# Joining the two recurrences of a bidirectional WKV layer into one scan, and moving the gate product one chunk later

## The reference, cut to what matters

```python
def step(carry, kv_t):                      # per channel, along T = 16384 tokens
    p, q, o = carry
    no = jnp.maximum(o, u + kt)
    A = jnp.exp(o - no); Bw = jnp.exp(u + kt - no)
    y = (A * p + Bw * vt) / (A * q + Bw)
    no2 = jnp.maximum(w + o, kt)
    A2 = jnp.exp(w + o - no2); B2 = jnp.exp(kt - no2)
    return ((A2 * p + B2 * vt, A2 * q + B2, no2), y)
...
k = jnp.einsum('btc,dc->btd', xs, Wk); v = ...Wv; r = ...Wr
x_fwd = wkv_scan(real_w, u, k, v)
x_bwd = jnp.flip(wkv_scan(real_w, u, jnp.flip(k, 1), jnp.flip(v, 1)), 1)
h = jax.nn.sigmoid(r) * 0.5 * (x_fwd + x_bwd)
h = layernorm(h) * ln_g + ln_b
out = jnp.einsum('btc,dc->btd', h, Wo)
```

## Time and profile before

| | us |
|---|---|
| median of 3 runs | 7379.21 |
| lowest, highest | 7375.27, 7381.88 |
| the profiled execution, its own time | 7389.65 |
| its span (first to last instruction) | 7388.1 |

### The profile page before, as it was taken

How to read it: one execution, slowest core, us unless ns; L and a number is a source line. 1 busy time by engine, 2 the same in 40 slices (tenths; PEclk the granted TensorE clock), 3 DMA queues, 4 the chain that set the end, 5 groups by cost and what they waited for, 6 DMA issues and landing times. The chain is left out here.

```text
span 7388.1 us, 83141 instructions
## 1 busy us (share of the span) xinstructions
PE 5742.4 (78%) x25278; PEld 2350.9 (32%) x25278; DVE 5654.6 (77%) x5545; ACT 2765.0 (37%) x3703; POOL 350.0 (5%) x553
## 2 busy tenths in 40 slices
PE   0999997999999564556665777688678879986888
PEld 0333332433333464333332222222222223222222
DVE  6333333999999777888885666599889979997998
ACT  0222222211111574111110000055479965546998
POOL 0111100000000000222220000000000000000000
PEclk9999999999999776777777877789789988877999
DMA  7556565999999996999997999644366644445665
GB/s 293 194 178 201 176 200 167 277 273 271 268 274 264 228 230 147 246 248 251 251 249 178 265 261 264 180 187 183 151 215 230 230 157 179 182 172 191 224 230 181
DMA packets 1208246, 1615.57 MB, mean 219 GB/s; under 512 B 87300, under 2 KB 907205, under 8 KB 1194693
## 3 DMA queue, kind: packets, MB, share of 16 engines
q1 hardware_dynamic: 865733, 1314.24, 59.3%
q10 hardware_dynamic: 314880, 201.39, 9.9%
q0 software_dynamic: 27520, 98.54, 5.2%
HBM read 1006.55 MB, written 607.33 MB: 218 GB/s over the span
## 5 line engine op out<-in xcount | busy, mean ns | idle before, releaser
L508 PE MATMUL dw_p<-dw_it,dw_tt 128*128 128x512 f32 x2304 | 1024.8, 606 | 122.6 <-DVE dw_tt L424 84.5
L547 DVE SCALAR_TENSOR_TENSOR dw_vo<-dw_vi,keep_wv,dw_vo 128x2048 f32<-128x2048 f32 x384 | 903.1, 2352 | 13.6
L842 PE MATMUL bc_p<-bc_z,bc_wc 128*32 128x256 f32 x9216 | 572.3, 414 | 399.9 <-DVE bc_z L881 399.9
L320 PE MATMUL pw_p<-pw_xh,pw_wlo 128*112 128x512 f32 x1536 | 693.2, 601 | 184.0 <-POOL pw_xh L274 184.0
L881 DVE STREAM_TRANSPOSE bc_z<-bc_xp 128x1536 f32<-128x1536 f32 x256 | 710.8, 2842 | 155.3 <-DMA bc_xp<-d 154.6
L1090 PE MATMUL ap_p<-ap_vt,ap_pw 96*96 96x512 f32 x1024 | 592.7, 744 | 191.5 <-DMA ap_xt<-in_x 187.0
L508 PEld LDWEIGHTS dw_p<-dw_it,dw_tt 128*128 128x128 f32 x2304 | 441.4, 193 | 706.1 <-issue 671.2
L525 ACT ACTIVATE dw_ot<-dw_p 128x512 f32<-128x512 f32 x384 | 215.6, 599 | 931.5 <-PE dw_p L508 663.7
L375 DVE COPY pw_ut<-pw_p 112x512 f32<-112x512 f32 x384 | 247.3, 686 | 379.5 <-PE pw_p L326 377.5
L842 PEld LDWEIGHTS bc_p<-bc_z,bc_wc 128*32 128x32 f32 x9216 | 323.9, 119 | 648.4 <-issue 486.5
L820 ACT ACTIVATE bc_xt<-bc_p 128x256 f32<-128x256 f32 x384 | 147.8, 385 | 873.9 <-PE bc_p L842 873.9
(11 more groups left out here) (313 smaller groups left out, 9826.6 us busy)
## 6 DMA issues: line engine op xcount, KB each, us to landing
u<-pw_ut SPq DMA_DIRECT2D x64, 2240.0 KB, 12.7
dw_it<-u SPq DMA_DIRECT2D x192, 512.0 KB, 10.8
d<-dw_ot ACTq DMA_DIRECT2D x192, 512.0 KB, 12.1
gr_qk<-d SPq DMA_DIRECT2D x128, 768.0 KB, 9.1
bc_xp<-d SPq DMA_DIRECT2D x256, 288.0 KB, 12.1
bc_xp<-d POOLq DMA_DIRECT2D x256, 288.0 KB, 9.9
gs_xt<-in_x SPq DMA_DIRECT2D x24, 2048.0 KB, 7.2
d<-dw_vo SPq DMA_DIRECT2D x96, 512.0 KB, 8.6
```

Of the source, the lines that this page charges most:

```text
L320: mm(pt[m % NBANK][e][:, :], wlo[:, wm], xh[:, h, 2 * e, cols], start=True, stop=False, skip_group_check=True)
L508: mm = nc.tensor.matmul(po[c][:, :].rearrange("p (b w) -> p b w", b=B), tt[:, h, 3 * c + dx, 0:H], it[:, h, B * c:B * (c + 1), dx:dx + W], ...
L547: nc.vector.scalar_tensor_tensor(vo[:, h], src, w, vo[:, h], ALU.mult, ALU.add).then_inc(tapped, 1)
L842: mm = nc.tensor.matmul(po[q % NBANK][32 * c4:32 * c4 + 32, :, :], wc[:, c, dx, :, :].rearrange("p j r -> p (j r)"), z[:, h, c, :, dx:dx + ...
```

## The change

In both functions the denominator's and the numerator's terms now lie in one buffer, [128, 3 tiles, 2, 512]: `bb` replaces `bl` and `bvl`, `fb` replaces `bf` and `bvf` and has one extra column per row (pitch 513), `sums` replaces `qq` and `pp`, `dn` replaces `den` and `num`. `ewt` holds the decay written out in full, [128, 3, 2, 513], with 0 in the extra column.

- One scan per chunk runs over all 6 x 513 = 3078 columns. At each extra column the factor 0 wipes the running value out and the carried start value is added in its place. One product of 6 columns replaces the two of `carry`.
- The sums with the bonus are three instructions of 2 x 512 columns. The rescaling on ACT is three ACTIVATEs of 2 x 512 columns.
- Backward: ACT evacuates `pv` with the bias added (three more ACTIVATEs), DVE multiplies b x v in SBUF instead of reading PSUM, and the bias matmuls (six pieces per chunk) go. b and b x v go to HBM with one DMA of twice the size, and forward loads them with one.
- The order of DVE's step changes: the scan, then y and b x v (backward) or `var`, the clamp, and the gate product of the chunk before (forward), and `dn` last.
- Forward: `rc`, y, the gate product `hh` and 1/den are handled for chunk n-2 in step n (before: n-1); `var`, `rs` and hh x rs for n-3 (before: n-2); the evacuation of `po` for n-4 (before: n-3). On ACT 1/den comes first, and exp(-r) nearly last. PE's order changes likewise: r, the residual, the mean of chunk n-2, the projection of n-3, the mean of the squares of n-2.

The core of the diff:

```diff
+def row(ap):
+    return ap.rearrange("p a b t -> p (a b t)")
+def spread_decay(nc, dve, ewt, ew, slot, spread):
+    for tile in range(3):
+        last = nc.vector.tensor_copy(ewt[:, tile].rearrange("p b t -> p (b t)"), ew[:, tile, :].to_broadcast([128, 2 * CH + 2]))
+    last.then_inc(spread, 1)
+    dve.wait_ge(spread, 1)
+    nc.vector.memset(ewt[:, :, :, slot:slot + 1], 0.0).then_inc(spread, 1)
+    dve.wait_ge(spread, 2)
+def carry(nc, dve, m, slots, ends, factor, scanned, carried):
+    if isinstance(m, int) and m == 0:
+        nc.vector.memset(slots, 0.0).then_inc(carried, 1)
+    else:
+        dve.wait_ge(scanned, m)
+        nc.vector.tensor_tensor(slots, ends, factor.rearrange("p (t a) -> p t a", a=1).to_broadcast([128, 3, 2]),
+                                ALU.mult).then_inc(carried, 1)
+    dve.wait_ge(carried, m + 1)
...
# wkv_backward, SP
-                    sp.dma_start(rows_of(b_d, c), flat(bl[:, h])).then_inc(b_stored[h], 16)
...
-                    sp.dma_start(rows_of(bv_d, c), flat(bvl[:, h])).then_inc(bv_stored[h], 16)
+                    sp.dma_start(rows_of(bb_d, chunk(n - 2)), bb[:, h].rearrange("p a b t -> p (a b t)")).then_inc(b_stored[h], 16)
...
# wkv_backward, PE
-                wait(pe, bv_done, n)
-                for tile in range(3):
-                    mm(pv[:, tile, :], vrow[:, tile, :], ones[:, :], start=True, stop=False, skip_group_check=True)
-                project(nc, pv, wv, xt[:, h], begin=False).then_inc(v_done, 1)
+                wait(pe, vv_done, n)
+                project(nc, pv, wv, xt[:, h]).then_inc(v_done, 1)
...
# wkv_backward, ACT (between fac and the rescaling)
+                    act.wait_ge(v_done, n + 1)
+                    for tile in range(3):
+                        last = nc.scalar.activation(bb[:, h, tile, 1, :], pv[:, tile, :], ACT.Identity, bias=vb[:, tile:tile + 1])
+                    last.then_inc(vv_done, 1)
                     act.wait_ge(f_done, n + 1)
                     act.wait_ge(b_done, n + 1)
+                    act.wait_ge(bv_done, n + 1)
+                    wait(act, dn_done, n - 1)
                     for tile in range(3):
-                        last = nc.scalar.activation(bf[:, h, tile, :], bl[:, h, tile, :], ACT.Copy, scale=fac[:, h, 1, tile:tile + 1])
...
+                        last = nc.scalar.activation(fb[:, h, tile, :, 0:CH], bb[:, h, tile, :, :], ACT.Copy,
+                                                    scale=fac[:, h, 1, tile:tile + 1])
...
# wkv_backward, DVE, after diff
+                if has(n, 1):
+                    dve.wait_ge(f_done, n)
+                    dve.wait_ge(fb_done, n)
+                    carry(nc, dve, n - 1, fb[:, g, :, :, CH], sums[:, :, :, 0], fac[:, g, 0, :], scanned, carried)
+                    wait(dve, dn_done, n - 1)
+                    nc.vector.tensor_tensor_scan(row(sums[:, :, :, :])[:, ::-1], row(ewt[:, :, :, :])[:, ::-1], row(fb[:, g])[:, ::-1],
+                                                 ewt[:, 2, 1, CH:CH + 1], ALU.mult, ALU.add).then_inc(scanned, 1)
                 if has(n, 2):
                     dve.wait_ge(rc_done, n - 1)
...
+                    nc.vector.tensor_tensor(yb[:, h], dn[:, :, 1, :], rc[:, :, :], ALU.mult).then_inc(y_done, 1)
+                if has(n):
+                    dve.wait_ge(vv_done, n + 1)
+                    dve.wait_ge(b_done, n + 1)
+                    nc.vector.tensor_tensor(bb[:, h, :, 1, :], bb[:, h, :, 1, :], bb[:, h, :, 0, :], ALU.mult).then_inc(bv_done, 1)
                 if has(n, 1):
...
+                        last = nc.vector.scalar_tensor_tensor(dn[:, tile], fb[:, g, tile, :, 0:CH], eu[:, tile, :],
+                                                              sums[:, tile, :, 1:CH + 1], ALU.mult, ALU.add)
+                    last.then_inc(dn_done, 1)
...
# wkv_forward, the new order on ACT (lag: has(n, lag))
#   lag 2  Ln(dn), Exp -> rc          lag 4  xo        lag 0  fac, fb
#   lag 3  lv, rs                     lag 1  sg: Ln, Exp
#   lag 2  hsq                        lag 0  sg: exp(-r)        lag 2  msq
# wkv_forward, the new order on DVE
#   lag 0  s, diff    lag 1  carry, scan    lag 3  var    lag 1  clamp of sg
#   lag 2  rc x num, + y, x sg -> hh        lag 3  hh x rs        lag 1  dn
+                    nc.vector.tensor_tensor_scan(row(sums[:, :, :, :]), row(ewt[:, :, :, :]), row(fb[:, g]), ewt[:, 0, 0, 0:1],
+                                                 ALU.mult, ALU.add).then_inc(scanned, 1)
...
+                    wait(dve, o_done, n - 3)
+                    nc.vector.tensor_tensor(flat(hh[:, h]), flat(rc[:, :, :]), flat(sg[:, h]), ALU.mult).then_inc(h_done, 1)
```

More of the change, by code:

```diff
@@ L1645, in step @@
                 if has(n, 2):
+                    act.wait_ge(dn_done, n - 1)
+                    wait(act, h_done, n - 2)
+                    nc.scalar.activation(rc[:, :, :], dn[:, :, 0, :], ACT.Ln).then_inc(ln_done, 1)
+                    act.wait_ge(ln_done, n - 1)
+                    nc.scalar.activation(flat(rc[:, :, :]), flat(rc[:, :, :]), ACT.Exp, scale=-1.0).then_inc(rc_done, 1)
+                if has(n, 4):
+                    act.wait_ge(o_done, n - 3)
+                    wait(act, stored[h], 64 * (t - 2))
+                    for tile in range(3):
+                        last = nc.scalar.activation(xo[:, h, tile, :], po[:, tile, :], ACT.Identity, bias=cb[:, tile:tile + 1])
+                    last.then_inc(ev_done, 1)
@@ new lines, in step @@
+                if has(n):
+                    act.wait_ge(d_done, n + 1)
+                    wait(act, carried, n - 1)
+                    wait(act, fb_done, n - 1)
+                    nc.scalar.activation(fac[:, h].rearrange("p a b -> p (a b)"), diff[:, h].rearrange("p a b -> p (a b)"),
+                                         ACT.Exp).then_inc(f_done, 1)
+                    act.wait_ge(b_loaded[h], 16 * (t + 1))
+                    act.wait_ge(f_done, n + 1)
+                    wait(act, dn_done, n - 1)
+                    for tile in range(3):
+                        last = nc.scalar.activation(fb[:, h, tile, :, 1:CH + 1], bb[:, h, tile, :, :], ACT.Copy,
+                                                    scale=fac[:, h, 1, tile:tile + 1])
+                    last.then_inc(fb_done, 1)
@@ new lines, in step @@
+                if has(n, 3):
+                    act.wait_ge(var_done, n - 2)
+                    nc.scalar.activation(lv[:, :], var[:, :], ACT.Ln, bias=eps[:, 0:1]).then_inc(lv_done, 1)
+                    act.wait_ge(lv_done, n - 2)
+                    wait(act, hn_done, n - 3)
+                    nc.scalar.activation(rs[:, 1, :], lv[:, :], ACT.Exp, scale=-0.5)
+                    for tile, lo in ((0, 0), (2, 64)):
+                        for p in (0, 64):
+                            last = nc.scalar.activation(rs[p:p + 64, tile, :], lv[lo:lo + 64, :], ACT.Exp, scale=-0.5)
+                    last.then_inc(rs_done, 1)
@@ L1761, in step @@
-                    last.then_inc(den_done, 1)
-                if has(n, 1):
-                    dve.wait_ge(bvf_done, n)
-                    scans(g, pp, bvf).then_inc(scanned, 1)
-                    dve.wait_ge(scanned, n)
-                    wait(dve, hs_done, n - 1)
-                    for tile in range(3):
-                        last = nc.vector.scalar_tensor_tensor(num[:, tile, :], bvf[:, g, tile, :], eu[:, tile, :],
-                                                              pp[:, g, tile, 0:CH], ALU.mult, ALU.add)
-                    last.then_inc(num_done, 1)
```

310 lines of the change are left out of this document (94 added, 216 removed).

## The result

The changed kernel takes 7190.33 us (median of 4 runs, 7185.45 to 7199.31) against 7380.55 for the kernel before in the same comparison: ratio 0.9739, interval 0.9719 to 0.9759, so 2.6% faster. A second comparison gave 0.9749 (0.9731 to 0.9767). I had predicted 7230, with a range from 7195 to 7315. The direction is right and so is the mechanism in the middle of the stages, but the result lies just under the range, and the term for the ends of the stages was wrong. One execution of the study, of the kernel with six scans, ran at a lower clock (granted 0.742, 7767.92 us) and is left out.

What follows compares the result with a forecast made beforehand. DVE was taken to bound all four last stages. Chunk savings of 162 us, less 8 at stage ends, gave 154, taken as 149 for extra waits: 7379 - 149 = 7230 us, range 7195 to 7315.

Steps and rivals of the forecast that it cites:

- ends of the stages: All four stages: 1/den no longer covered loses 12 us, backward prologues shed 4 in all; net 8 us lost.
- DVE as the bound: Last four stages: DVE busy 98.7% backward and 98.0% forward, so what leaves its stream shortens the chunk.
- The scan's split: DVE's scan: 211 ns fixed plus 2.064 ns a column, so the joined scan takes 6.56 us, 6.48 less overlap.
- What it saves: The joined scan on DVE saves fixed cost only: 0.84 us a chunk backward, 0.86 forward.
- Rival 3: DVE's scan costs by the column (7.54 us): 7366 us; half of that, or odd rows: 7300 to 7333; chance 0.09.
- Chunk distances: Backward 1.24 us less, period 15.84; forward 1.29 less, period 19.29; 162 us over 64 chunks each.
- What covers what: Other engines keep up: backward, ACT's added evacuation lies under the scan; forward, ACT has 1.1 us in hand.
- rival 2: ACT becomes forward's bound, period 20.0 to 20.4 us instead of 19.3: 7275 to 7300 us; chance 0.18.
- Rival 4: Forward, PE closes a ring and DVE waits before `var`; slower kernel, up to 7428 us; chance 0.06.
- 2.9 us in hand: Forward, PE's mean, projection and mean of the squares end by 22.9 us; `var` wants them at 25.8.
- waits of the new order: Extra waits caused by the new order were taken to lower the gain from 154 to 149 us.
- worth nothing because PE isn't the bound: Backward: removing PE's bias matmuls, 2.84 us a chunk, was claimed to save no time.

## Why the prediction was right, and where it was not

**DVE as the bound: right.** It is 99% busy in both windows, and each added instruction in its stream showed in the stages at its own size (six scans 69 us on DVE, 71 in the stages; six sums 50 and 50).

**The scan's split: right. What it saves: right in size, and only in part for the reason given.** The two lengths now measured give (6630 - 1268) / (3078 - 512) = 2.09 ns a column and 0.20 us fixed; I had worked out 2.064 and 0.211 from instructions of another kind. Predicted 6.56 us, measured 6.63; start to start 6.48 and 6.55. But of the 0.84 that I booked as fixed cost only 0.54 is that (the run with six scans); another 0.23 is the distance from scan to dependent sum, which sat unseen in the 7.32 of the earlier trace rows and went with the new order. Rival 3 is out, in both of its forms: a sum of 1024 columns over the pitch of 513 takes as long as predicted (3.59 for three, 3.6).

**Chunk distances: right within the last tenth.** Backward -1.20 where I had -1.24 (the scan's 0.07); forward -1.38 where I had -1.29; the 0.09 between them lies in several small parts. The 64 distances of each kind give 165 us, predicted 162.

**What covers what: right.** The evacuation of v on ACT and the rescaling are hidden backward, the bias matmuls were worth nothing in the middle (the run with the bias on PE), and ACT had 0.9 us in hand forward against my 1.1, so rival 2 did not occur, though it was near. Rival 4 did not occur either: no wait stands before `var` in forward's chunk. But my 2.9 us in hand there rest on a slip: I let the projection start at 15.1, with hh x rs, though PE's order puts the mean before it. From `hh` at 13.4 the three take 2.96 + 4.81 + 2.96 and end at 24.1, which leaves 1.7. Timeline of PE, the last matmul of the mean of the squares:

```profile
5691.58 0.59 PE L1581 MATMUL wf_pq<-wf_hsq,wf_one 128*64 128x512 f32 x1
```

It ends at 5692.17, and `var` starts at 5693.66, 1.5 us later. So the forecast held there with half the room that I had reckoned with.

ACT's waits backward are before the rescaling, as said (365.4 us in 64 waits for b x v, `fb` at L1398).

**The step that failed: "Ends of the stages".** I put them at 8 us lost and took 5 more off for waits of the new order. Measured, they gained 177.7 - 165.1 = 12.6 us: 20.6 us more than predicted, and the 5 us never came. Backward I had about -2 (4 shed in the prologues, 6 for the last 1/den) and 11.1 came; forward I had about -6 and 1.5 came. Two things I had counted are there. The first maximum of the backward stages comes 1.2 and 2.8 us earlier (I had 2 each), the second of these within what that prologue varies by. And at a backward stage's end the last 1/den lies open, timeline of DVE:

```profile
5269.71 1.76 DVE L1450 TENSOR_TENSOR wb_yb<-wb_dn,wb_rc 128x1536 f32<-128x1536 f32 x1 [3.06 <-ACT wb_rc L1406]
```

3.06 us where I had 3.1. What I had left out is the filling of the pipelines. I argued from the middle of a stage, where DVE is the bound, that PE's bias matmuls are "worth nothing because PE isn't the bound"; in the first two chunks of a backward stage DVE waits for PE, and there they and the old order did cost. The first two distances went from 14.16 and 18.51 to 9.68 and 14.14 us in the first backward stage and from 12.46 and 18.51 to the same in the second, 6.4 + 4.8 = 11.2 us beyond what any distance in the middle gained. Shown by experiment is PE's share, 7.8 of the 11.2 (the run with the bias on PE). The rest of the backward account, 4.0 from the prologues, 1.3 for ends that grew and 2.4 because a stage has only 31 distances between its 32 chunks, makes 11.5 against the 11.1 found.

Forward, the fill shortened too, but most of that is work put off. The first two distances went from 18.14 and 22.8 to 11.52 and 17.50 us, for the first of them no longer has the product, y and gate product of a chunk in it (5.3 us) and the second no hh x rs; both come one step later and are paid at the end. What did get earlier is the first scan: it started 43.8 us into the stage and now starts at 37.9 and 37.7. Timeline of DVE at that place, kernel before, kernel after, and the run with forward's old order:

```profile
5383.00 0.96 DVE L1752 TENSOR_SCALAR wf_sg<-wf_sg 128x1536 f32<-128x1536 f32 x1 [8.46 <-ACT wf_sg L1675]
```

```profile
5313.92 0.06 DVE L1266 MEMSET wf_fb<- 128x6 f32 x1 [3.02 <-ACT wf_fb L1643]
```

```profile
5331.23 0.96 DVE L1723 TENSOR_SCALAR wf_sg<-wf_sg 128x1536 f32<-128x1536 f32 x1 [7.63 <-ACT wf_sg L1645]
```

Before, the clamp of `sg` stood ahead of the first scan on DVE and waited for exp(-r); now the scan waits only for the rescaling. With the clamp ahead again the first scan starts at 43.4 and 42.9 us; with exp(-r) early on ACT and the clamp left behind the scan, at 37.9 and 37.6. So it is the clamp's place that counts. From the last scan to a forward stage's end it takes 61 us where it took 47.3, 13.6 more, and that takes nearly all of the fill's gain back. I had put 3.1 us of loss on each forward stage; measured, the two come out 1.5 us better in all.

**The range.** With the ends right, 7379 - 177.7 = 7201 would have stood just inside it. The rest, down to 7190, is not explained by the change and is chance as far as the traces tell: the first layer ended between 4718 and 4745 us in all the executions here, whatever the kernel. I had allowed no spread for it and set the low end by a faster scan alone.

## What to carry to other kernels

Cost each edit twice, once in the middle of a stage and once in the first two and the last chunks, where another engine is the bound: work that is free in the one can cost in the other, and a kernel of several stages pays it in each. When instructions are joined, ask what the shorter ones covered: in forward, joining the scans and sums paid only with the product a chunk later and the exponential moved, and without either the kernel was slower than before. A gain read off start-to-start distances can also hold waits for a result, which the order removes and not the joining. When a change touches some stages only, compare those stages and not the totals, for here an untouched one varied by more than the smaller effects.

## What the runs showed of the hardware

An instruction that needs a 6.63 us scan's result starts 0.27 us later than one that doesn't (6.82 against 6.55). Behind three scans of 512 columns it was 0.12 (3.67 forward) and 0.22 (3.77 backward) against 3.55.

GpSimd beside DVE was the surprise. Its product was recorded as 9.07 us (5006.18 to 5015.25), wholly over DVE's scan and b x v, and b x v ended at 5016.86, 1.6 us behind it, about its own length. So the lines fit engines that take turns: GpSimd behind the scan for 3.3 us, then b x v; the records call the standing still busy. The last product of each backward stage, with nothing on DVE beside it, took 3.42 us, so some 5.7 of the 9.07 are waiting. The Trainium skill ("SBUF — State Buffer", SBUF: two separate sides) says that the two share one pair of ports, held for a whole instruction by whichever comes first; the trace agrees with these numbers.

The untouched first layer differed by up to 27 us (0.6% of it) between executions of kernels that are the same there, while the four stages behind it repeated within about 1 us for one and the same kernel, and within about 3 where another part of the kernel had been edited.
